# Keys weighted and split with tokens on partitions and turned by a DMA, in a fused attention and feed-forward kernel on one core

## The chip, the cores and the metric

The kernel runs on one core of a Trainium2 chip. The metric is the device time of one execution in microseconds. Before the change it is 687.81 us, the median of three runs (687.43 to 687.95).

## The reference

A grouped convolution and a small mixture gate are followed by attention and a quantised feed-forward block. The part that the change touches is the attention over B = 32 samples of 32 tokens, seen as one sequence per sample, with 32 query heads in 8 groups that share a key and a value head of 128 elements:

```python
q = (x @ Wq.T).reshape(b, s, H, HD).transpose(0, 2, 1, 3)
k = (x @ Wk.T).reshape(b, s, HKV, HD).transpose(0, 2, 1, 3)
v = (x @ Wv.T).reshape(b, s, HKV, HD).transpose(0, 2, 1, 3)
q = _rmsnorm(q, q_norm_w)
k = _rmsnorm(k, k_norm_w)          # k * rsqrt(mean(k*k) + eps) * w
scores = jnp.einsum('bkgqd,bksd->bkgqs', qg, k) / math.sqrt(HD)
attn = jax.nn.softmax(scores + bias[None], axis=-1)
out = jnp.einsum('bkgqs,bksd->bkgqd', attn, v)
return out @ Wo.T
```

After it come gate, up and down projections with integer weights from which zero points are subtracted (`gint`, `uint`, `dints` in the kernel) and which are scaled afterwards.

## The kernel before

Every large product is made of three fp16 matmuls (high times high, high times low, low times high), `split_product` at L651 to L653. A float32 tile is split in two steps: ScalarE (ACT) writes the fp16 high half, and VectorE (DVE) or GpSimd (POOL) writes what is left as the low half.

Attention is cut into 16 units, `u` = 0 to 15. Two units, one for each half of the samples (`half` = u % 2), make one key head `kv`; they share the weights of that head. A unit is one call of `step` on each engine. All five engines have their own order, written out by hand, and meet at semaphores. On TensorE (PE) a unit runs: the scores of the unit before (48 small matmuls), three of four query blocks, the turn of the probabilities, the fourth query block, probabilities times values (L841), keys and values (`project_kv`), and then `finish`: four output blocks (`project_out`, 12 matmuls each, into the four banks PC) of the unit before, with the turn of this unit's keys (`transpose_k`, L798, four matmuls against the identity) after the second. An even unit also turns the maxima of the next weights (`maxima_rows`, L686) after the second output block and spreads them (`maxima_all`, L692) after the third; DVE works between the two (`maxima_diagonal`) and after (`maxima_powers`, `scale_wo`).

The keys of a unit take this way: ACT copies them from PSUM (`kraw`, L1200), squares them (`ksq`) and forms the mean (`kms`); POOL takes the power (`kinv`, L2121) and multiplies (`kn`, L2125); PE turns `kn` into the bank PB[0]; ACT scales by the norm weights, now one for each partition, and writes `khi` (L1234); DVE writes `klo` (L1666). `scores` waits for `d_klo`. In the order of ACT `keys_high` stands after `split_wkv`, in the order of DVE `keys_low` stands after the second output addition of `finish`.

Queries of the units from 2 on (`FIRST` = 2) already go another way: they are split with tokens on partitions, into `qpair`, and SP issues eight transposing DMAs for a unit (`turn_queries`, L583), each of 32 partitions and 16 blocks of 128 elements. Their norms travel by two small DMAs (`norms`, `qmoved`) and reach the scores in `scores_biased` on DVE.

SP's queue is one list for everything: integer loads, weight loads, query transposes, norms. DVE's order in a unit starts with the scores of the unit before and ends with the output additions; the integers of the down projection (`down_ints`, L1744) and the maxima of the integers (`ints_max`, L1750, two reductions) stand just ahead of `finish`. On POOL, `keys_values` is followed, in odd units, by `split_wq` (L2069, four subtractions) and `split_wkv`.

## Time and profile before

| | |
|---|---|
| median of 3 runs | 687.81 us |
| the profiled execution's own time | 686.33 us |
| its span | 684.5 us |
| PE busy | 665.2 us, 97% |
| DVE busy | 559.3 us, 82% |
| POOL busy | 453.5 us, 66% |
| ACT busy | 419.0 us, 61% |
| attention, two units | 58.37 us, in each of the five such stretches from 184 to 476 us |

The stages are about: the convolution and gate to 52 us, the first units to 112 us, the other units to about 491 us, a passage between attention and feed-forward to about 510 us, and feed-forward from there on. A busy share is an average over these stages. A timeline row gives an instruction's start, its duration, the engine, the line and the operands; what stands in brackets behind it is the idle time before it and what ended that. Matmuls are pipelined: 128x512 fp16 ones show 0.38 us each but start 0.22 us apart, and it is the distance between starts that counts.

### The profile page before, as it was taken

What the parts mean: (1) busy time and instruction counts of PE and PEld (TensorE: products, weight loads), DVE (VectorE), ACT (ScalarE), POOL (GpSimd) and SP (SyncE); (2) the same over time, 40 slices, a digit from 0 to 9 for tenths busy, and PEclk for the clock granted to TensorE, in tenths of its full rate; (3) what the DMA queues carried; (4) which work ended last, traced back from release to release, by engine and by line L of the source; (5) the groups of instructions that cost most, each with busy time, mean ns of one, the idle gap of its engine ahead of it and who ended that gap; (6) DMA issues with size and microseconds to landing.
All of it is one profiled execution on the core that took longest, in us unless ns stands there. A gap on an engine that the chain in (4) does not pass through costs nothing.

```text
span 684.5 us, 14468 instructions
## 1 busy us (share of the span) xinstructions
PE 665.2 (97%) x5004; PEld 374.7 (55%) x5004; DVE 559.3 (82%) x843; ACT 419.0 (61%) x1259; POOL 453.5 (66%) x379
## 2 busy tenths in 40 slices
PE   9999999999999999999999999999979999999995
PEld 8766555656656565665646656565634434444442
DVE  5867878969878887986977898677776899899987
ACT  0488572844647375474656638446465777877874
POOL 0468874873776497287559538737537678877886
PEclk9999999999999999999999999999999999999999
DMA  7420354574376366427426734443300156656454
GB/s 268 176 90 1 130 147 97 128 213 83 87 145 198 78 154 203 105 61 225 115 69 164 204 87 102 125 89 95 56 2 0 32 108 120 112 109 139 93 101 115
DMA packets 98800, 79.15 MB, mean 116 GB/s; under 512 B 79521, under 2 KB 80065, under 8 KB 96577
## 3 DMA queue, kind: packets, MB, share of 16 engines
q1 hardware_dynamic: 94864, 65.97, 36.7%
q0 software_dynamic: 3456, 12.58, 9.8%
q8 instruction: 24, 0.39, 0.2%
q14 instruction: 24, 0.19, 0.1%
q10 hardware_dynamic: 432, 0.01, 0.0%
HBM read 48.01 MB, written 2.21 MB: 73 GB/s over the span
## 4 chain that ended last, share of the span: by engine, by line
PE 65%; DVE 11%; POOL 10%; issue 7%; ACT 3%; DMA 3%; POOLq 0%; DVEq 0%; ACTq 0%
PE bank L651 17%; PE bank L653 17%; PE bank L652 17%; DMA acc<-dprod 3%; DVE exact L1945 3%; PE bank L703 2%; POOL wqlo L2069 2%; PE bank L841 1%; DVE mx L1533 1%; PE bank L1011 1%; PE bank L1012 1%; PE bank L995 1%; POOL qn L2105 1%; POOL whole L2193 1%; PE bank L1017 1%
## 5 line engine op out<-in xcount | busy, mean ns | idle before, releaser
L651 PE MATMUL bank<-wohi,oThi 128*128 128x512 f16 x256 | 97.1, 379 | 2.2 <-DVE oTlo L1721 2.1
L651 PE MATMUL bank<-wqhi,cThi 128*128 128x512 f16 x256 | 97.0, 379 | 0.9 <-POOL wqlo L2069 0.6
L653 PE MATMUL bank<-wohi,oTlo 128*128 128x512 f16 x256 | 97.0, 379 | 0.0
L652 PE MATMUL bank<-wolo,oThi 128*128 128x512 f16 x256 | 97.0, 379 | 0.0
L653 PE MATMUL bank<-wqhi,cTlo 128*128 128x512 f16 x256 | 97.0, 379 | 0.0
L652 PE MATMUL bank<-wqlo,cThi 128*128 128x512 f16 x256 | 97.0, 379 | 0.0
L1167 ACT ACTIVATE qraw<-bank 128x512 f32<-128x512 f32 x64 | 37.8, 591 | 81.5 <-PE bank L653 80.9
L2117 POOL TENSOR_TENSOR qinv<-qms,neghalf 128x8 f32<-128x8 f32 x28 | 56.9, 2030 | 39.6 <-ACT qms L1186 39.6
L2079 POOL TENSOR_TENSOR wolo<-wor,wohi 128x512 f16<-128x512 f32 x32 | 39.7, 1260 | 56.0 <-ACT wohi L1147 56.0
L1178 ACT ACTIVATE qsq<-qraw 128x128 f32<-128x128 f32 x256 | 75.4, 299 | 1.7
L1729 DVE SCALAR_TENSOR_TENSOR x<-bank,ysc,x 128x512 f32<-128x512 f32 x64 | 47.1, 744 | 30.6 <-PE bank L653 30.5
L1945 DVE SCALAR_TENSOR_TENSOR exact<-bank,uscl,exact 128x512 f32<-128x512 f32 x84 | 62.7, 746 | 10.5 <-ACT exact L1404 6.8
L651 PE MATMUL bank<-wkvhi,cThi 128*128 128x256 f16 x256 | 69.9, 273 | 0.0
L653 PE MATMUL bank<-wkvhi,cTlo 128*128 128x256 f16 x256 | 69.8, 273 | 0.0
L652 PE MATMUL bank<-wkvlo,cThi 128*128 128x256 f16 x256 | 69.8, 273 | 0.0
L2105 POOL TENSOR_TENSOR qn<-qraw,down 128x512 f16<-128x512 f32 x56 | 65.3, 1166 | 5.2 <-ACT qraw L1167 5.0
L2069 POOL TENSOR_TENSOR wqlo<-wqr,wqhi 128x512 f16<-128x512 f32 x32 | 37.8, 1213 | 25.9 <-ACT wqhi L1133 25.9
L1678 DVE SCALAR_TENSOR_TENSOR qn<-qraw,qn 128x512 f16<-128x512 f32 x56 | 46.4, 837 | 10.3 <-POOL qn L2105 10.2
L2198 POOL TENSOR_TENSOR whole<-whole,exact 128x512 f32<-128x512 f32 x27 | 36.2, 1339 | 21.7 <-DVE exact L1945 20.5
L1178 ACT ACTIVATION_READ_ACCUMULATOR qsq<-qraw 128x1 f32 x256 | 48.8, 191 | 0.0
L1017 PE MATMUL bank<-hT,dints 128*128 128x512 f16 x112 | 42.4, 379 | 2.5 <-DVE hT L1974 1.4
L1011 PE MATMUL bank<-fT,uint 128*128 128x512 f16 x112 | 42.6, 380 | 1.9 <-DVE whole L1934 1.7
(225 smaller groups left out, 1794.3 us busy)
## 6 DMA issues: line engine op xcount, KB each, us to landing
acc<-dprod POOLq DMA_DIRECT2D x24, 512.0 KB, 4.6
wqr<-in_wq SPq DMA_DIRECT2D x8, 1024.0 KB, 7.4
wor<-in_wo SPq DMA_DIRECT2D x8, 1024.0 KB, 6.0
raw<-in_gu_w SPq DMA_DIRECT2D x28, 256.0 KB, 3.2
zeros<-in_gu_z SPq DMA_DIRECT2D x28, 256.0 KB, 4.5
wkvr<-in_wkv SPq DMA_DIRECT2D x8, 512.0 KB, 7.2
raw<-in_dn_w SPq DMA_DIRECT2D x14, 256.0 KB, 2.7
zeros<-in_dn_z SPq DMA_DIRECT2D x14, 256.0 KB, 3.5
```

What stands on the lines that cost most here:

```text
L651: mm(o, ahi, bhi, start=start and k == 0, stop=False)
L652: mm(o, ahi, blo, start=False, stop=False)
L653: last = mm(o, alo, bhi, start=False, stop=stop and k == n - 1)
L1011: mm(o, uint[:, i, c, :], fThi[:, c, tokens(half)], start=True, stop=False)
L1017: mm(o, ints, hThi[:, n % (LAG + 1), :], start=True, stop=False)
L1178: A(qsq[:, t % 2, g, :], qraw[:, t, g, :], ACT.Square, accum_out=qss[:, g, t:t + 1]).then_inc(a_qss, 1)
L1678: V.scalar_tensor_tensor(qpair[:, t, 1, :, :], qraw[:, t, :, :], V_DOWN, qpair[:, t, 0, :, :], ALU.mult, ALU.subtract).then_inc(d_qlo, 1)
L1729: V.scalar_tensor_tensor(x[:, q, :], PC[t][:, :], ysc[:, half:half + 1], x[:, q, :], ALU.mult, ALU.add).then_inc(d_y, 1)
L1945: V.scalar_tensor_tensor(u, up_bank(n, c)[:, :], uscl[:, half, i, c:c + 1], u, ALU.mult, ALU.add).then_inc(d_us, 1)
L2069: Q.tensor_tensor(wqlo[:, c, :], wqr[:, c, :], wqhi[:, c, :], ALU.subtract).then_inc(p_wq, 1)
L2105: Q.tensor_tensor(qpair[:, t, 0, :, :], qraw[:, t, :, :], down[:, :, None].broadcast_to([P, G, HD]), ALU.mult).then_inc(p_qhi, 1)
L2117: Q.tensor_tensor(qinv[:, :, pair], qms[:, :, pair], neghalf[:, :, pair], ALU.pow).then_inc(p_qpow, 1)
```

## The change

In units 2 to 14 (`moved_keys`) the keys are handled with tokens on partitions all the way. The norm weights reach every partition as a row (`normw`, one more load; `wnrow`, one DVE instruction at the start). ACT no longer copies the keys; it squares them from PSUM. DVE multiplies them by `wnrow` out of PSUM into `kraw` (`keys_weighted`, two instructions a unit). POOL forms `kn` as before. ACT copies the high half and DVE subtracts for the low half, both into `kpair`, which is `kraw`'s memory seen as fp16. One transposing DMA a unit (128 partitions, 8 blocks of 128) writes `kT`, from which `scores` reads. The four PE transposes of these units are gone; units 0, 1 and 15 keep them.

Beside this, the maxima's two matmuls move into the middle of output blocks 2 and 3; DVE makes the keys' low half ahead of `down_ints`; `ints_max` moves from there to the next unit, behind `gate_ints`; ACT's `keys_high` goes ahead of `split_wkv` in odd units; and in SP's queue the load of `wor` and of the next head's first `up` integers move behind the loads of `wqr` and `wkvr`.

```diff
+        kpair = kraw[:, :, :].rearrange("p t d -> p (t d)").bitcast(F16).rearrange("p (t k d) -> p t k d", t=HQ, k=2)
-        khi = sb("khi", [P, HB, S], F16, att)
-        klo = sb("klo", [P, HB, S], F16, att)
+        kT = sb("kT", [P, HQ, 2, P], F16, att)
...
+        def moved_keys(u):
+            return not early_unit(u) and not (isinstance(u, int) and u == UNITS - 1)
...
+            sp.dma_start(normw[:, :, :], normw_in.rearrange("a (k d) -> a k d", k=2).broadcast_to([P, 2, HD])).then_inc(l_normw, 16)
...
                 turn_queries(u, 1, range(2, BQ))
+                if moved_keys(u):
+                    sp.wait_ge(d_klo, u + 1)
+                    sp.dma_start(kT[:, :, :, :].rearrange("p t k n -> p (t k) n"),
+                                 kpair.rearrange("p t k d -> p (t k) d"), transpose=True).then_inc(l_kT, 16)
                 sp.wait_ge(l_norms, 16 * n + 16)
...
             def scores(u):
-                pe.wait_ge(d_klo, u + 1)
+                if moved_keys(u):
+                    pe.wait_ge(l_kT, 16 * u - 16 * FIRST + 16)
+                else:
+                    pe.wait_ge(d_klo, u + 1)
...
-                    project_out(u - 1, 1 - half, kv if half else kv - 1, t)
-                    if t == 1:
+                    if not half and t >= 2:
+                        project_out(u - 1, 1 - half, kv - 1, t, range(2))
+                        if t == 2:
+                            maxima_rows(kv + 3, u)
+                        else:
+                            maxima_all(kv + 3)
+                        project_out(u - 1, 1 - half, kv - 1, t, range(2, G))
+                    else:
+                        project_out(u - 1, 1 - half, kv if half else kv - 1, t)
+                    if t == 1 and not moved_keys(u):
                         transpose_k(u)
...
             def keys_high(u):
+                if moved_keys(u):
+                    act.wait_ge(p_kn, u + 1)
+                    A(kpair[:, :, 0, :], kn[:, :, :], ACT.Copy).then_inc(a_khi, 1)
...
+            def keys_weighted(u, j):
+                dve.wait_ge(t_kv, 2 * u + j + 1)
+                dve.wait_ge(a_kss, HQ * u + 2 * j + 2)
+                if j == 0:
+                    dve.wait_ge(p_kn, u)
+                    dve.wait_ge(d_wnrow, 1)
+                    if u > FIRST:
+                        dve.wait_ge(l_kT, 16 * u - 16 * FIRST)
+                V.tensor_tensor(kraw[:, 2 * j:2 * j + 2, :], PA[j][:, :].rearrange("p (t w) -> p t w", t=2)[:, :, 0:HD],
+                                wnrow[:, None, :].broadcast_to([P, 2, HD]), ALU.mult).then_inc(d_kw, 1)
...
             def keys_low(u):
                 dve.wait_ge(a_khi, u + 1)
+                if moved_keys(u):
+                    V.tensor_tensor(kpair[:, :, 1, :], kn[:, :, :], kpair[:, :, 0, :], ALU.subtract).then_inc(d_klo, 1)
...
                 gate_ints(2 * kv - 1 if half else 2 * kv - 2)
+                if u > FIRST:
+                    ints_max(2 * kv - 2 if half else 2 * kv - 3)
```

On PE, in the output blocks of the even unit 2, there stood before (bank5 is output block 1, bank6 block 2, bank7 block 3; L798 turns keys):

```order
L653 MATMUL bank5<-wohi,oTlo 128x512
L798 MATMUL bank2<-const,kn 128x128 x4
L686 MATMUL bank0<-const,mx 4x128
L651 MATMUL bank6<-wohi,oThi 128x512
L652 MATMUL bank6<-wolo,oThi 128x512
```

and now stands:

```order
L674 MATMUL bank6<-wohi,oTlo 128x512
L709 MATMUL bank0<-const,mx 4x128
L672 MATMUL bank6<-wohi,oThi 128x512
L673 MATMUL bank6<-wolo,oThi 128x512
L674 MATMUL bank6<-wohi,oTlo 128x512
```

The keys' row is gone and the maxima have moved six matmuls on, into block 2; the spreading matmul (L692, now L715) sits in the same way in the middle of bank7.

On SP, in the odd unit 3 from the fourth query transpose on, there stood before:

```order
L583 DMA_TRANSPOSE qT<-qn 128x16x32 x3
L558 DMA wor<-in_wo 128x2048 [waits p_wo]
L583 DMA_TRANSPOSE qT<-qn 128x16x32 [waits d_qlo]
L583 DMA_TRANSPOSE qT<-qn 128x16x32
L594 DMA norms<-qinv 128x16 [waits d_qsc,p_qpow]
L583 DMA_TRANSPOSE qT<-qn 128x16x32 [waits d_qlo]
L583 DMA_TRANSPOSE qT<-qn 128x16x32
L598 DMA qmoved<-norms 32x4x4 [waits l_norms]
```

and now stands:

```order
L598 DMA_TRANSPOSE qT<-qn 128x16x32 x3
L598 DMA_TRANSPOSE qT<-qn 128x16x32 [waits d_qlo]
L598 DMA_TRANSPOSE qT<-qn 128x16x32
L609 DMA norms<-qinv 128x16 [waits d_qsc,p_qpow]
L598 DMA_TRANSPOSE qT<-qn 128x16x32 [waits d_qlo]
L598 DMA_TRANSPOSE qT<-qn 128x16x32
L613 DMA_TRANSPOSE kT<-kraw 128x8x128 [waits d_klo]
L617 DMA qmoved<-norms 32x4x4 [waits l_norms]
```

The load of `wor` has left the transposes, and the keys' transpose, which waits for DVE, stands between the queries' last one and the norms.

On DVE, in the odd unit 3, from the gate integers to the first matrices, and then around the values' low halves, there stood before:

```order
L1734 TENSOR_TENSOR gint<-raw,zeros 128x512
L1715 SCALAR_TENSOR_TENSOR pTlo<-bank,pThi 128x512
L1678 SCALAR_TENSOR_TENSOR qn<-qraw,qn 128x512
L1555 TENSOR_SCALAR wqr<-wqr,wup 128x2048
...
L1660 SCALAR_TENSOR_TENSOR vlo<-bank,vhi 128x256
L1744 TENSOR_TENSOR dints<-raw,zeros 128x512
L1750 TENSOR_REDUCE imax<-gint 128x1
L1750 TENSOR_REDUCE imax<-uint 128x1
L1729 SCALAR_TENSOR_TENSOR x<-bank,ysc,x 128x512 x2
L1666 SCALAR_TENSOR_TENSOR klo<-bank,wn,khi 128x512
```

and now stands (the low half of the keys is written into kraw's memory):

```order
L1815 TENSOR_REDUCE imax<-gint 128x1 [waits d_gint]
L1815 TENSOR_REDUCE imax<-uint 128x1 [waits d_uint]
L1780 SCALAR_TENSOR_TENSOR pTlo<-bank,pThi 128x512 [waits a_pThi]
L1743 SCALAR_TENSOR_TENSOR qn<-qraw,qn 128x512 [waits p_qhi]
L1600 TENSOR_SCALAR wqr<-wqr,wup 128x2048
...
L1713 TENSOR_TENSOR kraw<-bank,wnrow 128x256 [waits a_kss,t_kv]
L1722 SCALAR_TENSOR_TENSOR vlo<-bank,vhi 128x256 [waits a_vhi]
L1729 TENSOR_TENSOR kraw<-kn,kraw 128x4x128 [waits a_khi]
L1809 TENSOR_TENSOR dints<-raw,zeros 128x512 [waits l_dn]
L1794 SCALAR_TENSOR_TENSOR x<-bank,ysc,x 128x512 [waits d_y,t_y] x4
```

The two reductions now precede the probabilities' low half, and the keys' low half, with its wait for ACT, precedes the down integers and all output additions.

## Rows read from the trace of the kernel before

**Rows 1.** The page's first part: busy time of each engine.

```profile
PE 665.2 (97%) x5004; PEld 374.7 (55%) x5004; DVE 559.3 (82%) x843; ACT 419.0 (61%) x1259; POOL 453.5 (66%) x379
```

**Rows 2.** A stretch: length, then busy (count) of PE, PEld, DVE, ACT, POOL; clock, DMA.

```profile
242.73:301.10 58.37, 58.37 (x505) 33.93 (x507) 48.25 (x69) 33.64 (x126) 38.20 (x31) 1.00 0.51 136
```

**Rows 3.** Timeline of PE in odd unit 7, around the keys' turn.

```profile
253.66 0.38 PE L653 MATMUL bank<-wohi,oTlo 128*128 128x512 f16 x1
253.88 0.60 PE L798 MATMUL bank<-const,kn 128*128 128x128 f32 x4
254.31 0.38 PE L651 MATMUL bank<-wohi,oThi 128*128 128x512 f16 x1
```

**Rows 4.** Groups of PE instructions by line: the keys' turns of all 16 units.

```profile
L798 PE MATMUL bank<-const,kn 128*128 128x128 f32 x64 | 9.6, 273 | 0.0
```

**Rows 5.** Timeline of PE in even unit 8, around the spreading of the maxima.

```profile
285.72 0.38 PE L653 MATMUL bank<-wohi,oTlo 128*128 128x512 f16 x1
286.03 0.38 PE L692 MATMUL bank<-diag,spread 4*128 4x4 f32 x2
286.34 0.39 PE L651 MATMUL bank<-wohi,oThi 128*128 128x512 f16 x1
```

**Rows 6.** Timeline of POOL, ACT and DVE, odd unit 7: the way of the keys.

```profile
252.64 1.04 POOL L2125 TENSOR_TENSOR kn<-kraw,kinv 128x512 f32<-128x512 f32 x1
253.64 4.49 POOL L2069 TENSOR_TENSOR wqlo<-wqr,wqhi 128x512 f16<-128x512 f32 x4
...
254.51 0.69 ACT L1234 ACTIVATE khi<-bank,wn 128x512 f16<-128x512 f32 x1 [0.93 <-PE bank L798]
...
249.09 0.68 DVE L1739 TENSOR_TENSOR uint<-raw,zeros 128x512 f16<-128x512 int32 x1
249.69 0.41 DVE L1660 SCALAR_TENSOR_TENSOR vlo<-bank,vhi 128x256 f16<-128x256 f32 x1
...
255.23 0.75 DVE L1666 SCALAR_TENSOR_TENSOR klo<-bank,wn,khi 128x512 f16<-128x512 f32 x1 [0.41 <-ACT khi L1234]
```

**Rows 7.** The tiles qT and fT: duration on SP's queue, and time to landing.

```profile
L583 SPq DMA_TRANSPOSE qT<-qn x112: 1203/1280/2062, 96.8 to 486.5; - x112
DMA to landing us min/median/max: 2.7/2.8/6.1
...
L628 SPq DMA_TRANSPOSE fT<-fpair x16: 1175/1254/2817, 551.7 to 592.3; - x16
DMA to landing us min/median/max: 2.3/4.1/6.9
```

**Rows 8.** Timeline of SP's queue, odd unit 7.

```profile
252.69 2.53 SPq L583 DMA_TRANSPOSE qT<-qn  x2
256.35 1.75 SPq L598 DMA_DIRECT2D qmoved<-norms  x4
```

**Rows 9.** Timeline of PE: the first score matmul after unit 7 and after unit 8.

```profile
259.49 0.18 PE L811 MATMUL bank<-khi,qT 128*128 128x32 f16 x1
...
288.94 0.18 PE L811 MATMUL bank<-khi,qT 128*128 128x32 f16 x1
```

**Rows 10.** Timeline of POOL, even unit 8.

```profile
280.99 1.04 POOL L2125 TENSOR_TENSOR kn<-kraw,kinv 128x512 f32<-128x512 f32 x1
```

**Rows 11.** Timeline of POOL, DVE and PE in odd unit 9: integers, low probabilities, their use.

```profile
297.63 1.03 POOL L2105 TENSOR_TENSOR qn<-qraw,down 128x512 f16<-128x512 f32 x1
...
297.92 1.30 DVE L1734 TENSOR_TENSOR gint<-raw,zeros 128x512 f16<-128x512 int32 x1
299.71 0.69 DVE L1715 SCALAR_TENSOR_TENSOR pTlo<-bank,pThi 128x512 f16<-128x512 f32 x1 [0.49 <-ACT pThi L1259]
...
301.03 0.23 PE L841 MATMUL bank<-pThi,vhi 32*128 32x128 f16 x4
```

**Rows 12.** Timeline of DVE in odd unit 7: the maxima of the integers.

```profile
251.62 0.67 DVE L1750 TENSOR_REDUCE imax<-gint 128x1 f32<-128x512 f16 x1
252.22 0.67 DVE L1750 TENSOR_REDUCE imax<-uint 128x1 f32<-128x512 f16 x1
```

More of the change, by code:

```diff
@@ L136, in build @@
         down = sb("down", [P, 1])
+        wnrow = sb("wnrow", [P, HD])
+        normw = sb("normw", [P, 2, HD])
         hx = sb("hx", [P, MAXIMA])
@@ L331, in build @@
         l_qT = sem("l_qT")
+        l_kT = sem("l_kT")
+        l_normw = sem("l_normw")
+        d_wnrow = sem("d_wnrow")
+        d_kw = sem("d_kw")
         l_norms = sem("l_norms")
@@ L608, in _ @@
                 first, second = 2 * kv - 2, 2 * kv - 1
-                load_up(first)
+                if kv == 1:
+                    load_up(first)
                 load_down(first)
@@ L623, in _ @@
                     load_wq(kv + 2)
+                if kv + 1 < HKV:
+                    load_up(second + 1)
+                    load_wo(kv + 1)
             for t in range(HQ):
@@ L810, in scores @@
                     qhi, qlo = (qT[:, b // (2 * BQ), b % BQ, b // BQ % 2, k, :, :] for k in range(2))
-                    mm(o, qhi, khi[:, b, :], start=True, stop=False)
-                    mm(o, qhi, klo[:, b, :], start=False, stop=False)
-                    last = mm(o, qlo, khi[:, b, :], start=False, stop=True)
+                    khi, klo = (kT[:, b // BQ, k, S * (b % BQ):S * (b % BQ) + S] for k in range(2))
+                    mm(o, qhi, khi, start=True, stop=False)
+                    mm(o, qhi, klo, start=False, stop=False)
+                    last = mm(o, qlo, khi, start=False, stop=True)
                 last.then_inc(t_s, 1)
@@ L843, in apply_probs, with project_out @@
                 last.then_inc(t_pv, 1)
-            def project_out(u, half, kv, t):
+            def project_out(u, half, kv, t, groups=range(G)):
                 if half == 0 and t == 0:
@@ L852, in project_out @@
                     pe.wait_ge(d_oTlo, BQ * u + BQ)
-                split_product(PC[t][:, :], [(oThi[:, t, g, :, :], oTlo[:, t, g, :, :], wohi[:, g, :], wolo[:, g, :])
-                                            for g in range(G)], True, True).then_inc(t_y, 1)
+                last = split_product(PC[t][:, :], [(oThi[:, t, g, :, :], oTlo[:, t, g, :, :], wohi[:, g, :], wolo[:, g, :])
+                                                   for g in groups], 0 in groups, G - 1 in groups)
+                if G - 1 in groups:
+                    last.then_inc(t_y, 1)
             def mix(q):
@@ L895, in finish @@
                             transpose_q(u, tq)
-                    if not half and t == 1:
-                        maxima_rows(kv + 3, u)
-                    elif not half and t == 2:
-                        maxima_all(kv + 3)
             def first_project_q(u, half, t):
@@ L1197, in keys_values @@
                     act.wait_ge(t_kv, 2 * u + j + 1)
-                    if j == 0 and not first:
-                        act.wait_ge(p_kn, u)
-                    A(kraw[:, 2 * j:2 * j + 2, :], kv2[:, :, 0:HD], ACT.Copy).then_inc(a_kraw, 1)
+                    if not moved_keys(u):
+                        if j == 0 and not first:
+                            act.wait_ge(p_kn, u)
+                        A(kraw[:, 2 * j:2 * j + 2, :], kv2[:, :, 0:HD], ACT.Copy).then_inc(a_kraw, 1)
                     A(vhi[:, half, 2 * j:2 * j + 2, :], kv2[:, :, HD:2 * HD], ACT.Copy,
@@ L1206, in keys_values @@
                         act.wait_ge(a_kss, HQ * u)
-                    act.wait_ge(a_kraw, 2 * u + j + 1)
+                    if not moved_keys(u):
+                        act.wait_ge(a_kraw, keys_copied(u, j))
                     for t in (2 * j, 2 * j + 1):
-                        A(ksq[:, t, :], kraw[:, t, :], ACT.Square, accum_out=kss[:, t:t + 1]).then_inc(a_kss, 1)
+                        A(ksq[:, t, :], kv2[:, t % 2, 0:HD] if moved_keys(u) else kraw[:, t, :], ACT.Square,
+                          accum_out=kss[:, t:t + 1]).then_inc(a_kss, 1)
                 if 1 in pairs:
@@ L1290, in step @@
                     split_wq(kv + 1)
-                if half and not last:
+                    keys_high(u)
                     split_wkv(kv + 1)
@@ L1301, in step @@
                                       norms[:, :, g, :].rearrange("b s t -> s b t")).then_inc(l_qsc, 16)
-                keys_high(u)
+                if last or not half:
+                    keys_high(u)
                 if half and last:
@@ L1778, in finish @@
                         maxima_diagonal(kv + 3)
-                    if t == 1:
+                    if t == 1 and not moved_keys(u):
                         keys_low(u)
@@ L1818, in step @@
                     weight_max(M_O, wor, l_wo, kv).then_inc(d_mx, 1)
+                if moved_keys(u):
+                    keys_low(u)
                 down_ints(2 * kv - 1 if half else 2 * kv - 2)
-                ints_max(2 * kv - 1 if half else 2 * kv - 2)
+                if u == UNITS - 1:
+                    ints_max(2 * kv - 1)
                 if u == HQ:
@@ L2122, in keys_values @@
                 pool.wait_ge(p_kpow, u + 1)
-                if not (isinstance(u, int) and u == 0):
+                if moved_keys(u):
+                    pool.wait_ge(d_kw, 2 * u - 2 * FIRST + 2)
+                if isinstance(u, int) and 0 < u <= FIRST:
                     pool.wait_ge(t_kT, u)
+                elif not (isinstance(u, int) and u == 0):
+                    pool.wait_ge(d_klo, u)
                 Q.tensor_tensor(kn[:, :, :], kraw[:, :, :], kinv[:, :, None].broadcast_to([P, HQ, HD]),
```

36 lines of the change are left out of this document (25 added, 11 removed).

## The prediction

> **What bounds the kernel now.** I read the page's busy times first: TensorE (PE) is busy 97% of the span, DVE 82%, POOL 66%, ACT 61% [rows 1]. An average hides the stages, so I took the stretches next: in two attention units from 242.73 to 301.10 us PE is busy 58.37 of 58.37 us, at the full granted clock, while DVE has 10 us to spare and ACT and POOL 20 or more [rows 2]. PE is idle for none of it. So between about 112 and 491 us the time is what PE has in its queue: a PE instruction taken out is time saved, one for one, until another chain is late. The timelines then say which chains are near.
>
> **What goes from PE.** The four turns of the keys start at 253.88 and the next output matmul at 254.31: 0.43 us of PE's time [rows 3]. The group has 64 turns for 16 units [rows 4]; units 2 to 14 lose theirs. 13 x 0.43 = 5.6 us. The maxima's two matmuls stay. But the spreading one starts at 286.03, where the matmul before it began at 285.72 and, at the usual spacing of 0.22, left PE free at 285.94: 0.09 us of gap, and the whole takes until 286.34 [rows 5]. DVE's part in between gets the same four half blocks as before, plus the time of the two reductions that were in its way. Bounds: 0 and 0.3 us for each of seven even units; I take 0.07, the gap, so 0.5 us.
>
> **The way of the keys, odd units.** PE no longer waits for a turn, but `scores` now waits for a DMA. I work it out in unit 7. POOL ends `kn` at 253.68 [rows 6]. ACT's high half took 0.69 us out of PSUM; from SBUF I take the same, and 0.08 for the semaphore: 254.45. ACT is free for it, since it now stands ahead of `split_wkv`. DVE has nothing ahead of it but two more weightings of 256 elements (nearest row: `vlo`, 0.41 us each [rows 6]); they end near 252, so they cost nothing here. If ACT were later, they still would not. DVE's subtraction took 0.75 us when it read PSUM [rows 6]. Now both inputs are in SBUF, and POOL is then in its four subtractions (4.49 us, 1.12 each, 253.64 to 258.13) [rows 6]. An all-SBUF DVE instruction waits for POOL's to end: `gint` started at 297.92 beside a POOL multiplication that ended at 298.66 and took 1.30 us, where the same form (`uint`) takes 0.68 [rows 11, 6]. So the subtraction begins when POOL's first ends, at 254.76, and ends at 255.45; without the block it would end at 255.2. The Trainium skill (SBUF — State Buffer, section on the two separate sides) has this as an exclusive lock on a shared port pair, held for a whole instruction; by that rule, and the trace agrees, the block is at most one POOL instruction.
>
> SP gets to the keys' transpose in time: its last query transposes ended at 255.22 with the load of `wor` queued among them [rows 8], and that load is gone. How long a transpose of 128 partitions takes, no row shows. The nearest: 32 partitions and 16 blocks land 2.7 to 2.8 us after issue, 32 and 8 blocks 2.3 at the least [rows 7]. That is 0.4 us for 64 KB more; the keys' 256 KB are 128 KB more than a query transpose: 2.7 + 0.8 = 3.5 us. Below: 2.8, if the rows of 128 partitions spread better. Above: 5.6, twice a query transpose. I take 3.5, in line with the two rows. It lands at 255.5 + 3.5 = 259.0. PE wants the scores at 259.49 - 0.43 = 259.06 [rows 9]. There is no slack to speak of. One thing works for it: without the copies ACT gives POOL its means up to 0.3 us earlier. I take 0.1 us of wait for each of six odd units (3 to 13), 0.6 us; bounds 0 and 12.9 (2.15 each, at 5.6).
>
> **The way of the keys, even units.** In unit 8 `kn` ends at 282.03 and POOL then rests [rows 10]. 0.08 + 0.69 + 0.75 later, at 283.6, SP issues; 287.1 at 3.5 us. PE wants it at 288.94 - 0.43 = 288.5 [rows 9]. 1.4 us of slack, cost nothing; at 5.6 us it would be 0.7 late in each of seven.
>
> **What queues behind.** Behind the keys' transpose on SP stand the norms (`qmoved`), which DVE needs at once after the scores. They were issued from 256.35 to 258.10 [rows 8]; the transpose holds the queue 1.2 to 1.3 us, as those of both sizes do [rows 7], that is until 256.8, so they go 0.4 us later, while the `wor` load that competed with them is gone. Nothing for PE. Behind DVE's wait for the high half stand the down integers and the output additions; in odd units they start near 255.5 instead of 252.9, where the reductions ended [rows 12]. PE makes a block only every 2.6 us (12 x 0.22) and DVE adds one in under 1, so it catches up, and PE needs none of these banks before the next unit's values. SP asks for the down integers only after the norms. Nothing again.
>
> **The maxima of the integers.** They were two reductions of 0.67 us, 0.60 apart, so 1.27 us [rows 12], in a place with idle time behind it. Now they precede the probabilities' low half. In odd unit 9 `gint` ended at 299.22, DVE then idled 0.49 us, `pTlo` ran from 299.71 to 300.40, and PE used it at 301.03 [rows 11]. Now: 299.22 + 1.27 = 300.49, `pTlo` until 301.18, PE at about 301.25: 0.2 us late. Even units have no `out_scale` ahead of their integers; I count nothing for them. What comes before may also shift (`scale_wo` ends later, the POOL blocks fall elsewhere), by some tenths either way. Bounds 0 and 0.4 us for seven odd units; I take 0.15, 1.0 us.
>
> **The rest.** The weights' row is one small DVE instruction before the first scores, some tenths at most, and its load stands behind the input's in a queue that has to be empty for the second head's weights anyway. The feed-forward stage is untouched. Nothing.
>
> **The sum.** -5.6 - 0.5 + 0.6 + 1.0 = -4.5 us against the profiled execution's own 686.33 us (span 684.5): 681.8. The runs' median is 1.5 above that execution, so 687.81 - 4.5 = 683.3 us.
>
> **Rivals.**
> 1. *The keys' DMA is late in odd units, and the change is slower.* Place: `scores` after odd units. The place where it decides is 3.5 us from issue to landing. If SP's issue grows with the rows (2 x 1.28 instead of 1.28 us), it lands 4.8 us after issue, at 260.3: 1.25 us late, six times 7.5 us, instead of 0.6. The sum is then +2.4: 690.2 us. At 5.6 us it is 12.9 + 7 x 0.7 = 17.8 of wait, +12.7: 700 us. For it: no row has 128 partitions. Against: 8 and 16 blocks take 1.25 and 1.28 us on the queue [rows 7]. The Trainium skill (DMA: Bandwidth & Descriptors, the table of sequencer cycles in the section on why a DMA increments its semaphore by 16) gives for earlier generations a cost per tile of an SBUF transpose, so twice the tiles would be twice the issue; by that rule this rival is right, and rows 7 do not bear it out, since half the blocks cost the queue the same.
> 2. *DVE becomes late in odd units.* The 1.27 us push not only `pTlo` but also the query splits, `wqr` and the outputs' low halves. If nothing absorbs it, 0.8 us (1.27 - 0.49) appear in each of seven: 5.5 instead of 1.0, total 0: 687.8 us. For it: DVE has only 0.5 us of idle there [rows 11]. Against: the next DVE instruction waits for POOL in any case.
> 3. *Everything fits.* The transpose is as fast as a query's (2.8 us) and DVE's chain moves forward: -5.6 - 0.5 = -6.1, 681.7 us; with the whole bound of the maxima 680.1.
> 4. *The time does not move, since something other than PE holds the stage.* Then the turns' 0.43 us would reappear as PE idle. PE's idle time of 0 in rows 2 speaks against it; 687.8 us.
>
> **Chances.** Forecast (a few tenths of wait in odd units, 682 to 685.5): 0.50. Rival 3: 0.24. Rival 2: 0.09. Rival 4: 0.04. Rival 1: 0.13. A measurement of this kernel tells 0.2%, 1.4 us, from no change. Faster by more: the forecast, rival 3 and a little of rival 2, 0.76. Within: the rest of rival 2, rival 4 and a mild rival 1, 0.13. Slower: 0.11. The range reaches from 680.8 to 687.6 us; outside it are most of rival 1 and the last of rival 3. The likeliest case alone has 682 to 685.5.
>
> **What would show it.** Right: the keys' group of PE with 12 turns; stretches of two attention units near 57.5 us; a keys' transpose that lands 3 to 4 us after issue; PE idle before L842, if at all, only in odd units and below 0.3 us; before the first L872 of odd units 0.1 to 0.3 us, released by `pTlo`. Wrong: a landing above 4.5 us; idle time of PE before scores in even units; or the outputs' low halves as releaser of PE's output blocks.

## The result and the profile after

The changed kernel takes 683.57 us, the median of 7 runs (681.74 to 685.23), beside 687.95 us (687.43 to 688.85, 7 runs) for the kernel before on the same chip: ratio 0.9932, 95% interval 0.992 to 0.9944. The profiled execution took 682.99 us, its span is 681.2 us, 3.3 us less than the 684.5 us before. Two executions that ran at a lower granted clock, one of 699.98 us (experiment 6) and one of 1145.53 us (the kernel before, timed beside experiments 5 to 8), are left out of all medians.

The page's busy times, after:

```profile
PE 660.1 (97%) x4952; PEld 369.6 (54%) x4952; DVE 563.0 (83%) x870; ACT 411.2 (60%) x1233; POOL 458.0 (67%) x379
```

PE's busy time fell by 5.1 us, as its instructions did (52 turns are gone). Two stretches, after (columns as in [rows 2]): the window of [rows 2], and the time from the first scores of unit 2 to those of unit 15. The scores of a unit run on PE at the start of the step behind it, so "the scores of unit 7" are those that follow unit 7's keys.

```profile
242.73:301.10 58.37, 58.37 (x518) 33.66 (x505) 49.63 (x73) 33.05 (x125) 39.81 (x32) 1.00 0.57 145
115.03:486.34 371.31, 371.31 (x3183) 213.66 (x3182) 308.77 (x466) 211.78 (x796) 253.20 (x196) 1.00 0.59 140
```

The same stretch of units in the kernel before:

```profile
113.25:490.38 377.13, 376.62 (x3232) 219.30 (x3231) 306.71 (x439) 218.99 (x820) 249.07 (x196) 1.00 0.51 128
```

PE is not idle for any of the 371.31 us. The scores of an even unit follow those of the odd one before it by 29.01 us (29.45 in the kernel before), those of an odd unit by 28.49 (28.92): two units take 57.50 us instead of 58.37. Now the way of the keys. SP's transpose of the keys, after (minimum, median, maximum):

```profile
L613 SPq DMA_TRANSPOSE kT<-kraw x13: 1231/1231/2838, 110.8 to 454.3; - x13
...
DMA to landing us min/median/max: 3.0/3.1/4.7
```

Unit 7 and then unit 8, timelines of POOL, ACT, DVE, SP and PE, after, to be read beside [rows 6, 8, 9, 5]:

```profile
250.11 1.00 POOL L2191 TENSOR_TENSOR kinv<-kms,neghalf 128x4 f32<-128x4 f32 x1
251.33 1.04 POOL L2199 TENSOR_TENSOR kn<-kraw,kinv 128x512 f32<-128x512 f32 x1 [0.22 <-POOL kinv L2191]
252.33 5.41 POOL L2139 TENSOR_TENSOR wqlo<-wqr,wqhi 128x512 f16<-128x512 f32 x4
...
252.40 0.63 ACT L1275 ACTIVATE kraw<-kn 128x512 f16<-128x512 f32 x1 [0.75 <-POOL kn L2199]
...
253.07 0.97 DVE L1729 TENSOR_TENSOR kraw<-kn,kraw 128x512 f16<-128x512 f32 x1 [2.43 <-ACT kraw L1275]
...
254.07 1.23 SPq L613 DMA_TRANSPOSE kT<-kraw  x1
255.34 2.02 SPq L617 DMA_DIRECT2D qmoved<-norms  x4
...
258.51 0.18 PE L842 MATMUL bank<-kT,qT 128*128 128x32 f16 x1
...
281.24 0.69 DVE L1729 TENSOR_TENSOR kraw<-kn,kraw 128x512 f16<-128x512 f32 x1
...
281.96 1.23 SPq L613 DMA_TRANSPOSE kT<-kraw  x1
...
285.59 0.38 PE L674 MATMUL bank<-wohi,oTlo 128*128 128x512 f16 x1
285.90 0.38 PE L715 MATMUL bank<-diag,spread 4*128 4x4 f32 x2
...
287.52 0.18 PE L842 MATMUL bank<-kT,qT 128*128 128x32 f16 x1
```

In unit 7 the low half takes 0.97 us beside POOL's `wqlo` (0.69 in unit 8, where POOL rests). From issue to scores there are 258.51 - 254.07 = 4.44 us; the transpose needs 3.1, so 1.3 us are spare. (Where PE did wait for it, in experiments 3 and 10, the scores began 0.2 us after the landing, so some 1.2 of them are free.) In unit 8 the scores follow at 287.52, 5.56 after issue: 2.4 us spare. The first of these units have less. The transpose of unit 4 took longest to land:

```profile
167.43 2.84 SPq L613 DMA_TRANSPOSE kT<-kraw  x1
...
172.53 0.18 PE L842 MATMUL bank<-kT,qT 128*128 128x32 f16 x1
```

It landed 4.7 us after issue, 0.4 us ahead of its scores. Units 2, 3 and 5 had 1.0, 0.9 and 1.0 us between landing and scores; in a second execution of the same kernel units 2 to 5 had 0.5, 0.3, 0.3 and 0.9.

Odd unit 9's start, DVE and PE, after, beside [rows 11]:

```profile
295.92 1.30 DVE L1799 TENSOR_TENSOR gint<-raw,zeros 128x512 f16<-128x512 int32 x1
297.14 0.67 DVE L1815 TENSOR_REDUCE imax<-gint 128x1 f32<-128x512 f16 x1
297.74 0.67 DVE L1815 TENSOR_REDUCE imax<-uint 128x1 f32<-128x512 f16 x1
298.33 0.68 DVE L1780 SCALAR_TENSOR_TENSOR pTlo<-bank,pThi 128x512 f16<-128x512 f32 x1
...
299.61 0.23 PE L872 MATMUL bank<-pThi,vhi 32*128 32x128 f16 x4
```

`pTlo` is ready at 299.0, 0.6 us ahead of its use. The first scores of all, however, come later: 59.47 us after against 57.23 before. DVE, POOL, ACT and PE there, after:

```profile
51.09 1.18 DVE L1679 SCALAR_TENSOR_TENSOR wnrow<-normw,wcol 128x128 f32<-128x128 f32 x1
52.20 1.22 DVE L1681 TENSOR_TENSOR wn<-wcol 128x1 f32<-128x1 f32 x1
...
51.09 1.04 POOL L2199 TENSOR_TENSOR kn<-kraw,kinv 128x512 f32<-128x512 f32 x1
52.08 5.97 POOL L2128 TENSOR_TENSOR mixp<-mixw,le 128x512 f32<-128x512 f32 x4
...
53.45 1.08 ACT L1283 ACTIVATE qT<-bank 128x512 f16<-128x512 f32 x2 [1.99 <-DVE wn L1681]
...
54.07 1.29 DVE L1737 TENSOR_TENSOR qT<-bank,qT 128x512 f16<-128x512 f32 x2 [0.66 <-ACT qT L1283]
...
55.51 0.63 PE L825 MATMUL bank<-const,kn 128*128 128x128 f32 x4 [1.23 <-DVE qT L1737]
```

DVE before:

```profile
50.27 0.16 DVE L1633 TENSOR_TENSOR wn<-wcol 128x1 f32<-128x1 f32 x1
```

The span then adds up from score to score: start +2.24 us (59.47 - 57.23); units 0 and 1 up to the scores of unit 2 -0.46 (55.56 against 56.02); units 2 to 14 -5.82 (371.31 against 377.13); the rest +0.74 (194.86 against 194.12). Together -3.3 us. The last term belongs to this execution: from 495 to 500 and from 500 to 505 us its granted clock was 0.92 and 0.74, where the kernel before had 1.00. A second execution of the changed kernel (experiment 12) had 1.00 there and 193.84 us for the rest, 0.3 less than before.

### The profile page after: what moved, and what is told of

It reads as the page before. It is cut to its first block, busy times and chain, and to the rows that moved or that the text cites. A ratio compares the mean times of both kernels' runs of the same rounds, so it can differ in the third digit from the quotient of the medians.

```text
span 681.2 us, 14436 instructions
## 1 busy us (share of the span) xinstructions
PE 660.1 (97%) x4952; PEld 369.6 (54%) x4952; DVE 563.0 (83%) x870; ACT 411.2 (60%) x1233; POOL 458.0 (67%) x379
## 4 chain that ended last, share of the span: by engine, by line
PE 65%; DVE 10%; POOL 8%; issue 6%; DMA 6%; ACT 4%; SPq 0%; POOLq 0%; DVEq 0%; ACTq 0%
PE bank L672 18%; PE bank L673 18%; PE bank L674 18%; DMA acc<-dprod 5%; DVE exact L2015 3%; PE bank L726 2%; PE bank L872 2%; POOL wqlo L2139 2%; POOL whole L2267 1%; POOL whole L2272 1%; DVE acc L2037 1%; DVE part L2004 1%; PE bank L856 1%; PE bank L843 1%; PE bank L844 1%
## 5 line engine op out<-in xcount | busy, mean ns | idle before, releaser
L2149 POOL TENSOR_TENSOR wolo<-wor,wohi 128x512 f16<-128x512 f32 x32 | 42.6, 1352 | 58.0 <-ACT wohi L1184 58.0
L2187 POOL TENSOR_TENSOR qinv<-qms,neghalf 128x8 f32<-128x8 f32 x28 | 53.5, 1912 | 39.4 <-ACT qms L1223 39.4
L2175 POOL TENSOR_TENSOR qn<-qraw,down 128x512 f16<-128x512 f32 x56 | 66.8, 1193 | 2.8 <-ACT qraw L1204 2.8
L2139 POOL TENSOR_TENSOR wqlo<-wqr,wqhi 128x512 f16<-128x512 f32 x32 | 43.2, 1381 | 26.7 <-ACT wqhi L1170 26.7
L1184 ACT ACTIVATE wohi<-wor 128x512 f16<-128x512 f32 x32 | 17.5, 618 | 48.4 <-DVE wor L1606 48.4
L1743 DVE SCALAR_TENSOR_TENSOR qn<-qraw,qn 128x512 f16<-128x512 f32 x56 | 41.5, 750 | 5.2 <-POOL qn L2175 4.9
```

What stands on the lines that cost most here:

```text
L2139: Q.tensor_tensor(wqlo[:, c, :], wqr[:, c, :], wqhi[:, c, :], ALU.subtract).then_inc(p_wq, 1)
L2149: Q.tensor_tensor(wolo[:, g, :], wor[:, g, :], wohi[:, g, :], ALU.subtract).then_inc(p_wo, 1)
L2175: Q.tensor_tensor(qpair[:, t, 0, :, :], qraw[:, t, :, :], down[:, :, None].broadcast_to([P, G, HD]), ALU.mult).then_inc(p_qhi, 1)
L2187: Q.tensor_tensor(qinv[:, :, pair], qms[:, :, pair], neghalf[:, :, pair], ALU.pow).then_inc(p_qpow, 1)
```

## The experiments

Each was timed beside the kernel before, and its ratio is to that. Comparisons with the changed kernel are between medians: 683.57 us, and 682.58 us when it was timed again beside experiments 9 to 11, so differences under 1 us are not told apart. The changed kernel's ratio has the interval 0.992 to 0.9944. Those of experiments 2, 3, 4, 8 and 10 lie clear of it; those of 1, 6, 7, 9, 11 and 12 overlap it, and what is said of these rests on their profiles. Experiment 5 changes the kernel before and is compared with that. "Scores 2 to 15" is the time in the profile from the scores of unit 2 to those of unit 15 (changed kernel: 371.31).

**1. The weights' row made later.**

```diff
-                dve.wait_ge(l_normw, 16)          # score_scale, ahead of wn
-                V.scalar_tensor_tensor(wnrow[:, :], ...)
+            # the same two lines behind the first unit's add_outputs
```

> The changed kernel with the weights' row (wnrow) made after the first unit's outputs instead of ahead of wn. Theory (the row's DVE instruction took 1.18 us there and the next one 1.22, against 0.16 before, because both waited for POOL, and ACT's first turned queries wait for wn): the first scores come 1.4 us earlier, the whole 1.2 to 1.6 us faster than the changed kernel, about 682.2 us. Rival (the later start of the changed kernel is only how its input DMAs landed in that execution): no difference.

Measured: 681.67 us (680.42 to 683.21, 6 runs), ratio 0.9916 (0.9898 to 0.9933). DVE and PE in this kernel:

```profile
51.49 0.16 DVE L1678 TENSOR_TENSOR wn<-wcol 128x1 f32<-128x1 f32 x1
...
54.51 0.60 PE L825 MATMUL bank<-const,kn 128*128 128x128 f32 x4
...
84.73 0.34 DVE L1947 SCALAR_TENSOR_TENSOR wnrow<-normw,wcol 128x128 f32<-128x128 f32 x1
```

`wn` takes 0.16 us again and PE's wait of 1.23 us is gone. The row itself, at its new place with POOL idle, takes 0.34 us. First scores are at 58.44. The start also moves between executions, whatever the edit: the DVE instruction behind `scale` begins between 50.27 and 51.50 us in all fourteen profiles. From there to the first scores there are 8.4 us in each of the ten with the row at its first place, 6.95 in the three with none there and `wn` free, and 7.1 in one where `wn` alone met POOL. So the row costs 1.4 of the 2.24 us, and the other 0.8 are in how this execution began. The times alone do not tell the two kernels apart.

**2. The turns put back on PE.**

```diff
+                    elif t == 1:
+                        pe.wait_ge(d_pTlo, u)
+                        for c in range(HQ):
+                            nc.tensor.transpose(PB[0][:, P * c:P * c + P], ident, ident)
```

> The changed kernel with four turns of the identity on PE in units 2 to 14, where the turns of the keys stood, read by nobody. Theory (the stage is bound by PE alone, a turn of four costs 0.43 us): 13 x 0.43 = 5.6 us slower than the changed kernel, about 689.2 us. Rival (part of the gain came from the DMA way or from the moved DVE work, which stay): less than 4 us slower.

Measured: 689.45 us (686.94 to 690.44, 12 runs), ratio 1.0013 (0.9997 to 1.0029): 5.9 us more than the changed kernel. Scores are 28.92 and 29.45 us apart again, 0.43 more a unit, and PE has no wait at the turns. The units' gain is PE's 52 turns; the other edits together bring nothing that the times show.

**3. The keys' transpose behind the norms in SP's queue.**

```diff
+                sp.wait_ge(l_norms, 16 * n + 16)
+                for g in range(G if u < UNITS - 1 else 2):
+                    sp.dma_start(qmoved[...], norms[...]).then_inc(l_qsc, 16)
                 if moved_keys(u):
                     ...
                     sp.dma_start(kT[...], kpair..., transpose=True).then_inc(l_kT, 16)
-                sp.wait_ge(l_norms, 16 * n + 16)
-                for g in range(G if u < UNITS - 1 else 2): ...
```

> The changed kernel with the keys' transposing DMA issued after the four small DMAs of the norms, about 1.8 us later in odd units. Theory (in odd units the keys land 3.1 us after an issue at 254.07 and PE wants them at 258.51, so there are 1.3 us of slack, and 3.5 in even units): about 0.4 us of PE idle before the scores in each of six odd units, none in even ones, 2 to 3 us slower. Rival (the prediction's reckoning, no slack in odd units): 1.8 us in each of six, 10 us slower.

Measured: 691.65 us (690.15 to 692.75, 6 runs), ratio 1.0054 (1.0036 to 1.0071), 8 us more: far over my 2 to 3, and nearer to the rival's 10. Scores 2 to 15: 380.05. SP, and the tile's waits, in this kernel:

```profile
259.97 2.00 SPq L613 DMA_DIRECT2D qmoved<-norms  x4
262.02 1.23 SPq L616 DMA_TRANSPOSE kT<-kraw  x1
...
265.31 0.18 PE L842 MATMUL bank<-kT,qT 128*128 128x32 f16 x1 [0.52 <-DMA kT<-kraw]
...
  PE bank L842: 6.4, 8
```

The transpose waits for the 2.0 us of the norms. In units 7, 9 and 11 PE is 0.7 us late, as the slack says: the issue comes 3.52 us after `kn` instead of 1.70, 1.8 later against 1.2 free. Even units from 6 to 12 do not wait. The miss lies in units 3, 4, 5 and 13, which take 1.9, 2.0, 1.0 and 1.4 us more, and 0.9 in unit 2. In 3, 5 and 13 that is a longer wait (1.74, 0.86, 1.26 us). In unit 4 it is the granted clock, which fell 1.9 us after the end of the wait of 1.74 us; the stretches there in this kernel:

```profile
146.66:150.00 3.34, 3.33 (x55) 2.05 (x56) 1.88 (x3) 0.00 (x0) 0.00 (x0) 0.78 0.87 166
150.00:155.00 5.00, 5.00 (x20) 2.04 (x19) 2.61 (x6) 2.28 (x10) 2.46 (x3) 0.80 0.98 396
155.00:160.00 5.00, 5.00 (x27) 2.56 (x26) 4.69 (x8) 4.42 (x20) 4.24 (x4) 1.00 0.83 309
```

A mean of 0.8 is some time at the lower of the two levels (1.2 GHz) and the rest at 2.4; eight matmuls there start 0.43 us apart instead of 0.22. So here a long wait of PE was followed by a loss of its own length once more. It happened once: the wait of 1.3 us in unit 4 of experiment 10 was followed by no fall. My sum took one settled odd unit for all.

**4. The maxima back between the output blocks, in the changed kernel.**

```diff
-                    if not half and t >= 2:
-                        project_out(u - 1, 1 - half, kv - 1, t, range(2))
-                        ...                       # maxima_rows or maxima_all
-                        project_out(u - 1, 1 - half, kv - 1, t, range(2, G))
+                    project_out(u - 1, 1 - half, kv if half else kv - 1, t)
+                    if not half and t == 1:
+                        maxima_rows(kv + 3, u)
+                    elif not half and t == 2:
+                        maxima_all(kv + 3)
```

> The changed kernel with the maxima's two matmuls back between output blocks (after the second and third). Theory (the 0.09 us gap before the spreading matmul is there in both places, and the one long wait for DVE's diagonal, 0.5 us in unit 4 of the kernel before, came from the sums that DVE makes there): within 0.6 us of the changed kernel. Rival (the prediction's term, 0.07 us for each of seven): 0.5 us slower, spread over seven units.

Measured: 686.2 us (684.68 to 687.13, 12 runs), ratio 0.9976 (0.9965 to 0.9986), 2.6 us more than the changed kernel; scores 2 to 15: 374.23, 2.9 more. More than either theory. Unit 8 in this kernel, DVE and PE:

```profile
281.22 2.27 DVE L1574 TENSOR_REDUCE mx<-wor 128x1 f32<-128x2048 f32 x1
...
283.44 0.38 PE L674 MATMUL bank<-wohi,oTlo 128*128 128x512 f16 x1
283.83 0.27 PE L709 MATMUL bank<-const,mx 128*4 128x128 f32 x1
...
272.45 0.24 PE L872 MATMUL bank<-pThi,vhi 32*128 32x128 f16 x4 [0.21 <-DVE pTlo L1776]
```

The spacing at L709 is 0.39 instead of 0.22 us: PE waits for `mx` of `wor`, which ends at 283.49, 6.0 us ahead of the scores at 289.53. In unit 14, where it ends 6.7 us ahead, nothing is lost. In the kernel before it ended 7.6 us ahead of them (288.94):

```profile
279.03 2.27 DVE L1533 TENSOR_REDUCE mx<-wor 128x1 f32<-128x2048 f32 x1
```

Units 8, 10 and 12 take 0.44 us more each, with this wait and one of 0.21 us for `pTlo`; units 3 to 5 take 0.43, 0.60 and 0.37 more. Why `pTlo` comes late here was not tested. In the changed kernel the maximum of `wor` ends 6.3 us ahead of the scores, 1.4 nearer than before. Of that the two weightings ahead of it account for 0.66 us (between `uint` and the maximum DVE had 0.67 us of work and now has 1.33), the turns that no longer stand between it and the scores for 0.43, and the integers' maxima, moved ahead of it, for some 0.2 (in experiment 6 it ends 6.46 ahead). The move into the blocks gives DVE 1.3 us more (six matmuls) to bring the maximum.

**5. The same move alone, in the kernel before.**

```diff
-                    project_out(u - 1, 1 - half, kv if half else kv - 1, t)
+                    if not half and t >= 2: ...   # as in the change
```

> The kernel before with one edit of the change alone: the weights' maxima (transpose and spreading matmul) stand amid output blocks 2 and 3, not behind blocks 1 and 2. My theory: alone it can give back only the 0.09 us gap per even unit and the one wait of TensorE in unit 4 (0.51 us, for the diagonal), so 0.6 to 1.1 us: 687.0 to 687.7, ratio 0.9982 to 0.9990. In the changed kernel it was worth 2.6 us since there DVE's maximum of wor ends later. Rival (it is worth the same wherever it stands): 685.6 us, ratio 0.9963. The other side: the reciprocals come later for wor, DVE's scale_wo then meets the scores' work, 689 us.

Measured: 687.44 us (686.3 to 689.37, 12 runs) against 687.93, ratio 0.9998 (0.9985 to 1.0011), so no gain that the times show. Scores 2 to 15: 376.55, 0.58 less than before, all of it the one wait in unit 4, which in the kernel before stood as

```profile
169.29 0.38 PE L692 MATMUL bank<-diag,spread 4*128 4x4 f32 x2 [0.51 <-DVE diag L1539]
```

The units' period is unchanged, so the 0.09 us gap of [rows 5] is no gain; it stands in the changed kernel as well (285.59 to 285.90).

**6. The integers' maxima at their old place.**

```diff
-                if u > FIRST:
-                    ints_max(2 * kv - 2 if half else 2 * kv - 3)
...
-                if u == UNITS - 1:
-                    ints_max(2 * kv - 1)
+                ints_max(2 * kv - 1 if half else 2 * kv - 2)
```

> The changed kernel with one edit undone: the two maxima of a chunk's integers (imax, 0.67 us each) stand behind the down integers again, not ahead of the probabilities' low half. My theory: the profile after shows no wait of TensorE for pTlo in odd units, it is made 0.6 us before it is used, so the move costs nothing (I had reckoned 1.0 us) and undoing it gains nothing: behind the down integers DVE has idle time. 683.0 to 684.2 us, ratio to the kernel before 0.992 to 0.995. Rival A (my prediction's term was there and only covered by something else): 682.6 us or less, a gain of 1.0. Rival B (the move is what brings the powers and the normed keys forward on POOL): a wait of TensorE ahead of odd scores of 0.3 us or more, 685.5 us or more.

Measured: 683.49 us (682.49 to 685.29, 5 runs), ratio 0.9944 (0.9922 to 0.9966). From unit 5 on the scores are 28.49 and 29.01 us apart, as with the move, with no wait for `pTlo`. In units 3 and 4 they are not: the stretch 2 to 15 is 372.03, 0.7 more, with one wait of 0.43 us for the diagonal at 171.82. The runs can't tell 0.7 us.

**7. The low half behind the down integers.**

```diff
-                if moved_keys(u):
-                    keys_low(u)
                 down_ints(2 * kv - 1 if half else 2 * kv - 2)
+                if moved_keys(u):
+                    keys_low(u)
```

> The changed kernel with DVE's keys' low half behind the down integers instead of ahead of them. My theory: the keys' transpose has slack of 1.3 us in odd and 2.4 us in even units. In odd units DVE idles 2.43 us ahead of the low half, and the down integers (0.69 us) fit there; they can push POOL's normed keys by some 0.5 us at most. In even units the low half is 0.6 us later. Both within the slack: 683.0 to 684.2 us, no wait of TensorE ahead of scores. Rival (the order is what keeps the keys in time): 0.3 to 0.6 us of wait in each odd unit, 686 us or more.

Measured: 682.75 us (681.99 to 684.55, 6 runs), ratio 0.9931 (0.9911 to 0.9951); scores 2 to 15: 371.32. In even units issue-to-scores fell from 5.56 to 5.28 us; PE saw nothing.

**8. The load of `wor` back among the query transposes.**

```diff
                 turn_queries(2 * kv + 1, 0)
+                if kv + 1 < HKV:
+                    load_wo(kv + 1)
                 later_queries(2 * kv + 1)
...
                     load_up(second + 1)
-                    load_wo(kv + 1)
```

> The changed kernel with the load of wor (1 MB) back among the query transposes, ahead of the keys' transpose, in SyncE's queue of odd units. My theory: the load and its data delay the last query transposes by about 1.2 us (in the kernel before they ended at 255.2 in unit 7, in the changed kernel at 253.8), and the keys' transpose with them; the slack is 1.3 us, so TensorE waits between 0 and 0.5 us in some of the odd units: 683.6 to 686 us. Rival A (the landing also grows, since 1 MB shares the DMA engines): landing above 4 us and a wait of 1 us or more in each of six, 689 us or more. Rival B (the load's place is without effect): 683.6 us and an issue of the keys' transpose that does not move.

Measured: 685.06 us (683.59 to 688.69, 12 runs), ratio 0.9969 (0.9954 to 0.9985): 1.5 us more. Scores 2 to 15: 372.59, 1.3 more. Unit 7 of this kernel on SP, and PE in unit 5:

```profile
253.17 2.53 SPq L598 DMA_TRANSPOSE qT<-qn  x2
255.74 1.34 SPq L613 DMA_TRANSPOSE kT<-kraw  x1
...
202.38 0.18 PE L843 MATMUL bank<-kT,qT 128*128 128x32 f16 x1 [0.74 <-DMA kT<-kraw]
```

Once settled the keys go 4.0 to 4.4 us ahead of the scores (4.4 before). The load holds the queue for 0.58 us, yet the query transposes behind it move only 0.25 to 0.3 us towards the scores: the queue had been waiting there for DVE's low half. The cost is in units 5 and 6, which take 0.9 and 0.2 us more. The size agrees with my range, the place does not.

**9. ACT's high half behind the split of the key and value weights.**

```diff
                     split_wq(kv + 1)
-                    keys_high(u)
                     split_wkv(kv + 1)
+                    keys_high(u)
```

> The changed kernel with ACT's keys' high half behind the split of the key and value weights in odd units, as it stood in the kernel before. My theory: ACT idles 0.75 us ahead of the high half, the split (1.13 us for two) takes that place and makes the high half 0.35 us later, well inside the slack of 1.3 us: 683.0 to 684.2 us. Rival (the place ahead of the split is needed): a wait of TensorE of 0.3 us or more in each of six odd units, 685.5 us or more.

Measured: 682.71 us (681.65 to 684.12, 5 runs), ratio 0.9918 (0.9903 to 0.9933), beside 682.58 for the changed kernel timed with it. No wait in odd units from 7 on, one of 0.36 us in unit 3; scores 2 to 15: 372.36, 1.0 more, all of it in units 3 and 5, which the medians can't tell.

**10. The keys 2 us later.**

```diff
                     act.wait_ge(p_kn, u + 1)
+                    for i in range(3):
+                        act.wait_ge(a_spare, 3 * (u - FIRST) + i)
+                        A(spare[:, :, :], kn[:, :, :], ACT.Copy).then_inc(a_spare, 1)
+                    act.wait_ge(a_spare, 3 * (u - FIRST) + 3)
                     A(kpair[:, :, 0, :], kn[:, :, :], ACT.Copy).then_inc(a_khi, 1)
```

> The changed kernel with three spare copies on ACT ahead of the keys' high half in units 2 to 14 (0.63 us each and the semaphore between them, 2.1 us together). They change nothing but how late the keys are. It measures the slack of the keys' transpose. My theory (1.3 us of slack in odd units, 2.4 in even ones): TensorE waits 0.5 to 1.2 us ahead of the scores of each of six odd units and hardly in even ones, 3 to 7 us together: 686.5 to 691 us. Rival A (no slack, as my prediction had it): 2.1 us in odd units and 0.7 and more in even ones, 17 us, 700 us. Rival B (what follows takes the delay up, since the next unit's keys start later too): below 685.5 us.

Measured: 694.08 us (693.52 to 694.88, 5 runs), ratio 1.0093 (1.0078 to 1.0108); scores 2 to 15: 381.87, 10.6 more. An odd and an even unit of this kernel, DVE and PE:

```profile
259.75 1.14 DVE L1735 TENSOR_TENSOR kraw<-kn,kraw 128x512 f16<-128x512 f32 x1 [4.50 <-ACT kraw L1281]
...
264.22 0.18 PE L844 MATMUL bank<-kT,qT 128*128 128x32 f16 x1 [1.01 <-DMA kT<-kraw]
...
289.01 0.69 DVE L1735 TENSOR_TENSOR kraw<-kn,kraw 128x512 f16<-128x512 f32 x1 [2.01 <-ACT kraw L1281]
...
291.85 0.22 DVE L1590 TENSOR_SCALAR diag<-const,rowmax 4x4 f32<-4x4 f32 x1
...
292.12 0.38 PE L717 MATMUL bank<-diag,spread 4*128 4x4 f32 x2 [0.44 <-DVE diag L1590]
```

The odd units came as reckoned: 1.0 us of wait in each from unit 5 on (0.77 in unit 3), that is 2.1 plus 0.2 of a longer subtraction less 1.3 of slack. That shows the slack. The 10.6 us are still 3.6 over the top of my figure, since in even units the delay reaches PE another way than by the DMA: DVE waits 2.0 us for ACT, and the maxima's diagonal, behind it in DVE's order, is 0.44 us late (1.3 in unit 4).

**11. Row late and down integers first.** Both edits of 1 and 7.

> The changed kernel with two edits that did not harm it singly: the weights' row is made after the first unit's output additions, and DVE takes the down integers ahead of the keys' low half. My theory: the row's edit gives its 1.4 to 1.9 us again, the other nothing that TensorE sees: 681.3 to 682.3 us, ratio to the kernel before 0.990 to 0.992. Rival (they add up, since the down integers move into DVE's idle time): 680.8 us or less.

Measured: 682.03 us (680.74 to 684.55, 6 runs), ratio 0.9916 (0.9897 to 0.9934), the same as row late alone; the two edits do not add up. It is 0.55 us below the changed kernel timed with it, which the runs can't tell. I would keep row late: it is faster than before by 0.84%. That it beats the changed kernel the profiles show (1.4 us at the start); its median is 1.9 us lower, but the ratios' intervals overlap.

**12. The changed kernel once more.** No edit.

> The changed kernel itself, beside the other three on one chip. Theory: 683.0 to 684.2 us, ratio to the kernel before 0.992 to 0.9945, and scores that start within 0.5 us of the first profile's. If the start of the input's loads differs again by 0.8 us between executions, the first scores move by that, with no edit made.

Measured: 682.58 us (680.75 to 683.84, 6 runs), ratio 0.9923 (0.9905 to 0.994); the time is 0.4 us under my range. First scores at 59.78, scores 2 to 15 again 371.31 to the hundredth.

## Why the prediction was right, point by point

- *What bounds the kernel* (PE's queue, one for one). Right: PE has no idle time in 371.31 us, and putting the turns back costs 5.9 us (experiment 2), 5.2 of them between the scores of units 2 and 15.
- *-5.6 us for the turns.* Right: 12 of the 13 units are 5.2 of the 5.82 us, the thirteenth is the 0.46 ahead of unit 2.
- *-0.5 us for the maxima.* The amount is right and its cause wrong. The seven gaps of 0.09 us stayed; what went is a single wait of 0.5 us in unit 4, with 0.58 in the stretch (experiment 5). What I did not see is that the change needs the move. The maximum of `wor` now ends 1.4 us nearer to the scores, by the two weightings ahead of it and the turns that are gone, and without the new place that costs 2.6 us (experiment 4). I weighed the move on the kernel before, where it is worth next to nothing.
- *+0.6 us of wait in odd units, "no slack to speak of".* Mis-sized; 0 was measured, with 1.3 us of slack. Two numbers make it: the landing took 3.1 us where I took 3.5, and `kn` came earlier. From its end to the scores there were 5.81 us before (259.49 - 253.68), 5.38 without the turn, and there are 6.14 now (258.51 - 252.37): 0.76 gained. I had named the earlier mean (0.3 us) and counted none of it. POOL's two powers between that mean and `kn` are shorter too, 1.95 and 1.00 us instead of 2.18 and 1.33. Experiments 3 and 10 find the 1.3 us from the other side. (My upper bound was also added up wrongly: 255.5 + 5.6 - 259.06 is 2.0 us late, not 2.15, so 12.2 us for six units, not 12.9, and rival 1's worst case is 699 us, not 700. The forecast does not use it.)
- *The block by POOL.* Right: 0.97 against 0.69 us, and the low half ends 1.67 us after `kn`, where I had 1.77.
- *Even units, 1.4 us of slack.* The transpose has 2.4 from unit 6 to 12. But my check asked only whether the DMA is late. The nearest wait in even units is DVE's maxima chain (experiment 10).
- *+1.0 us for `pTlo` behind the integers' maxima.* Mis-sized; no wait, 0.6 us of slack. The bound 0 to 0.4 us was right, the value taken was not: I kept 299.22 for the end of `gint`, but it now ends 2.0 us earlier, at 297.2, while PE's use is only 1.4 us earlier. `gint` met POOL in both kernels (1.30 us). What got shorter is an addition in the scores ahead of it, which meets POOL's `wolo` for less time, before and after:

```profile
291.06 1.66 DVE L1700 TENSOR_TENSOR sc<-sc,const 128x512 f32<-128x512 f32 x1
...
289.68 0.86 DVE L1765 TENSOR_TENSOR sc<-sc,const 128x512 f32<-128x512 f32 x1
```

  That another edit will leave this so is not shown. Undoing the move costs nothing in settled units (experiment 6).
- *"The weights' row is one small DVE instruction, some tenths at most".* This step failed: 1.4 us. I priced its work (0.34 us where POOL rests), not its place. In [rows 11] I had read that a DVE instruction in SBUF waits for POOL's and had used it for the large subtraction; at the start the row and `wn` each meet one of POOL's (`kn` and `mixp`) and take 1.18 and 1.22 us, where `wn` took 0.16, and ACT and PE stand behind them.
- *The signs.* I had called a landing above 4.5 us a sign of being wrong. One came, 4.7 us in unit 4, and did no harm: the issue was 5.1 us ahead of the scores. No odd unit waited for `pTlo`.

So the forecast's 683.3 us is close to 683.57 by luck in part, by two errors that cancel: 1.6 us of waits that did not come, and 1.4 us of start that I had at nothing. With both set right the sum is -6.1 + 1.4 = -4.7. The rival "everything fits" was the true account of the units; experiment 1, which takes the row's cost away, comes to its time (681.7 us forecast, 681.67 measured). Rivals 1, 2 and 4 fell with 3.1 us of landing, 0.6 us of slack at `pTlo` and zero idle time.

Still open: why units 2 to 6 are sensitive in experiments 3, 6, 8 and 9 while later ones hardly are. Part of it is that units 2 to 5 have 0.3 to 1.0 us between landing and scores where later odd units have 1.4 and even ones 2.5, and how much changes from one execution to the next. Why they have less, no run isolates.

## What to carry to other kernels

When one engine is full, price a removed instruction at its spacing, and then walk every chain that ends at that engine, not only the one that the edit touches: here the keys had slack, while the maxima's diagonal, a few instructions further in DVE's order, had less. Test each edit of a bundle in the kernel that has the others; the maxima's move is worth nothing that the times show alone and 2.6 us in the change. And a tiny instruction on the first chain of a kernel is priced by what it may stand behind.

## What the runs showed of the hardware

- A DVE instruction on one element of each partition, with both inputs in SBUF (`wn`), took 1.22 us behind a POOL instruction begun 0.1 us before it. In the four profiles without the row, `wn` and POOL's `kn` begin within 0.01 us of each other; three times `wn` took 0.16 us and once 1.05. The Trainium skill (SBUF — State Buffer, section on the two separate sides) speaks of an exclusive lock between the two engines; the trace agrees, and adds that a small instruction is not spared: the 128x1 one lost 1.06 us, the 128x512 `gint` of [rows 11] 0.62.
- A transpose of 128 partitions with 8 blocks (256 KB) holds SP's queue for 1.23 us and lands after 3.1 us (medians of 13); 32 partitions with 16 blocks (128 KB) take 1.28 and 2.8 [rows 7]. Twice the data costs 0.3 us. The rule of the Trainium skill on a cost per tile for earlier generations (DMA: Bandwidth & Descriptors, the section on why a DMA increments its semaphore by 16), by which the queue would be held twice as long, is not borne out.
- The passage between attention and feed-forward, where PE waits several times, had a granted clock of 0.92 and 0.74 in one execution and 1.00 in another of the same kernel, with 1.0 us of difference in the rest. Over all profiles the rest took 193.6 to 194.2 us in the six without such a fall, 194.2 to 194.8 in seven with one, and 197.3 in one with a second fall at 671 us; so the first fall cost at most some 1 us. The seven runs of the changed kernel have mean clocks from 0.995 to 0.999; the slowest, 685.23 us, had 0.995, and the fastest, 681.74, had 0.999.
